# Gated delta rule and FP4 feed-forward layer: the triangular matrices of the chunk solve change layout by 32x32 block transposes on VectorE instead of over DRAM

## The chip, the cores and the metric

The kernel runs on one core of a Trainium2 chip. The metric is the time on the device in microseconds (us) of one execution; lower is better. A core has five engines with a queue of instructions each: TensorE (PE, matrix products; its weight loads are PEld), VectorE (DVE), ScalarE (ACT), GpSimd (POOL) and SyncE (SP, which here only issues DMAs). Each works through its queue in order; semaphores tie them together.

## What is computed

The reference takes x of shape (2, 4096, 512), normalizes each row, and adds to x the outputs of two branches. The first is an attention of 16 heads with a gated delta rule, a recurrence over 4096 steps; the second a feed-forward part with FP4 weights:

```python
def step(S, inp):
    q_t, k_t, v_t, g_t, b_t = inp
    S = S * jnp.exp(g_t)[..., None, None]
    mem = jnp.einsum('bhk,bhkv->bhv', k_t, S)
    delta = (v_t - mem) * b_t[..., None]
    S = S + jnp.einsum('bhk,bhv->bhkv', k_t, delta)
    o_t = jnp.einsum('bhk,bhkv->bhv', q_t, S)
    return (S, o_t)
...
h = jax.nn.silu(gate) * up
y = jnp.einsum('bsi,hi->bsh', h, w_down)
rms = jnp.sqrt(jnp.mean(y * y, axis=-1, keepdims=True) + EPS)
...
xn = _layernorm(x, axis=-1)
x = x + _L0_attn_ref(xn, ...) + _L0_ffn_ref(xn, ...)
```

Before the recurrence, q, k and v pass a causal convolution of 4 taps and a SiLU, q and k are scaled to unit length, and g and beta come from x by small projections. After it, o is normalized per head, gated, and multiplied by o_w.

## The kernel before

A **tile** is 128 positions of both batch entries (NB = 2), so there are 32 tiles. Within a tile the recurrence is done in 4 chunks of 32 positions (CH = 32, NC = 4). For each of the 2 x 4 x 16 = 128 combinations of batch entry, chunk and head there is a 32 x 32 unit triangular matrix, and its inverse T is needed. The inverses are computed on GpSimd with one of the 128 combinations on each partition.

The work is a software pipeline over tiles. One **step** of each engine does the front of a tile n (projections, convolution, keys, gram products, solve, the whole feed-forward part) and the rest of the recurrence for the tile t before it. `run` gives every engine the same steps: the first has no t, the last, the 33rd, has no n. Each engine's order within a step is written out by hand.

The path of the triangles, with the lines of the profile:

- TensorE forms the gram products `gram(0)` and `gram(1)` (L1354). VectorE's `gram_products(b)` multiplies them with the decays: L987 writes the matrix for the solve into `kbq` (signal a_done), L988 writes D. Here a partition holds one position j of a chunk, and along the row are the 16 heads and 32 positions i: the **row layout**.
- SyncE writes kbq to DRAM, `scr_a` (L393), and reads it back into `la` in pieces of 16 partitions (L399), 2 x (1 + 4) issues per tile. In `la` a partition is one combination of batch entry, chunk and head, and holds the whole 32 x 32 matrix: the **head layout**.
- GpSimd's `solve` (L494 to L515) clears `lt`, waits for la, and does 31 steps of a product (L511) and a subtraction (L515). Its last signals t_done. Behind it in GpSimd's queue is `feed_forward_scale` (L525, L527), which turns ScalarE's sums of squares (L813) into the scale yr.
- SyncE writes lt to `scr_t` (L411) and reads it into `tT`, back in row layout (L417), 1 + 8 issues per tile.
- TensorE's `t_times_r` (L1221) of the next step uses tT as weights. It waits for the reads (t_read) and for out_done.

`la`, `tT` and the half `knq[1]` share the first 1024 columns of the tile `arena`; `lt` and `qk_rows` share the next 1024.

In the feed-forward part TensorE computes units u = 0 to 21 (L1153, L1154) and then products `down(m)` (L1166). ScalarE takes a unit from PSUM (L613), VectorE adds three scaled parts to it (L893, three per unit), ScalarE applies SiLU (L624), VectorE multiplies (`hidden`, L905). TensorE's unit(u) waits with its first half until VectorE's second L893 of unit(u-2) is done, with its second half for the third. Units 0 to 4 are interleaved with the gram products. At the end of a step VectorE forms the result in `obuf` (L1071, once per batch entry, after yr), which signals out_done, and begins the next step with the copy of the halo (L995), for which ScalarE's L600 waits, and behind that L593, which empties the banks of TensorE's projections (L1122).

## Time and profile before

| | before |
|---|---|
| median of 3 runs | 3328.89 us |
| lowest and highest | 3327.97, 3332.89 us |
| span of the profiled execution | 3330.7 us |
| TensorE busy | 3142.1 us (94%) |
| VectorE busy | 2390.6 us (72%) |
| GpSimd busy | 1918.8 us (58%) |
| ScalarE busy | 1667.4 us (50%) |
| chain that ended last | TensorE 77%, VectorE 12%, issue 6%, GpSimd 2%, DMA 1% |

The span goes from the first to the last instruction of the profiled execution; its own time was not given apart from it. It lies 1.8 us above the median of the runs. "Busy" on TensorE is occupancy, not its peak rate. Idle time of an engine costs something only if another one that is late waits for it.

### The profile page before, as it was taken

To read this page: it belongs to the slowest core of one execution; us is meant where nothing else is said; L and a number is where in the kernel's file an instruction comes from. 1 tells how busy PE (TensorE), PEld (TensorE's weight loads), DVE (VectorE), ACT (ScalarE), POOL (GpSimd) and SP (SyncE) were. 2 spreads that over 40 slices of the span, in tenths; PEclk is the share of its full clock that TensorE was granted. 3 is DMA by queue.
4 is the path that set the end of the run, shared out by engine and by line. 5 is a ranking of instruction groups with operands and counts; after the bars stand their busy time and mean duration, and the time that the engine had idled before them with its cause. 6 is when DMAs were issued, how large, how long until landed. Compare 5 with 4: busy or idle time off the path is not lost.

```text
span 3330.7 us, 118645 instructions
## 1 busy us (share of the span) xinstructions
PE 3142.1 (94%) x45632; PEld 2252.9 (68%) x45632; DVE 2390.6 (72%) x5408; ACT 1667.4 (50%) x3306; POOL 1918.8 (58%) x2865
## 2 busy tenths in 40 slices
PE   5999999999999999999999999999999999999995
PEld 4666766766666766666767767667667666767663
DVE  7677776777776777777777767777767777767772
ACT  3544554544554545554445545445545455544452
POOL 4566555666555665556665556665556655556652
PEclk8999999999999999999999999999999999999996
DMA  3111111111111111111111111111111111111111
GB/s 112 39 46 27 37 43 33 46 45 28 34 43 36 46 37 27 43 37 42 46 27 37 43 33 46 46 27 37 43 33 46 40 28 39 42 37 46 34 25 30
DMA packets 318318, 132.08 MB, mean 40 GB/s; under 512 B 277089, under 2 KB 278881, under 8 KB 317793
## 3 DMA queue, kind: packets, MB, share of 16 engines
q1 hardware_dynamic: 313824, 119.26, 14.3%
q8 instruction: 383, 6.28, 0.8%
q10 hardware_dynamic: 4096, 6.42, 0.5%
q14 instruction: 15, 0.11, 0.0%
HBM read 75.30 MB, written 50.33 MB: 38 GB/s over the span
## 4 chain that ended last, share of the span: by engine, by line
PE 77%; DVE 12%; issue 6%; POOL 2%; ACT 1%; ACTq 1%; DMA 1%; DVEq 0%; SPq 0%; POOLq 0%
PE PS L1166 17%; PE PS L1122 13%; PE PS L1153 8%; PE PS L1235 7%; PE PS L1154 7%; PE PS L1376 6%; DVE arena L893 4%; PE PS L1221 3%; PE PS L1300 2%; PE PS L1253 2%; DVE arena L378 2%; PE PS L1271 2%; PE PS L1391 2%; DVE arena L988 1%; PE PS L1178 1%
## 5 line engine op out<-in xcount | busy, mean ns | idle before, releaser
L893 DVE SCALAR_TENSOR_TENSOR arena<-PS,sc,arena 128x256 f32<-128x256 f32 x2112 | 1001.0, 482 | 253.0 <-ACT arena L613 152.2
L1153 PE MATMUL PS<-xh,wgu 128*128 128x256 f32 x2816 | 871.6, 341 | 35.9 <-DVE arena L893 35.4
L613 ACT ACTIVATE arena<-PS,sc 128x256 f32<-128x256 f32 x704 | 330.0, 474 | 759.0 <-PE PS L1154 700.3
L1154 PE MATMUL PS<-xl,wgu 128*128 128x256 f32 x2816 | 698.8, 282 | 0.0
L1166 PE MATMUL PS<-wdn,inner 128*128 128x512 f32 x1408 | 650.7, 592 | 0.0
L1153 PEld LDWEIGHTS PS<-xh,wgu 128*128 128x128 f32 x2816 | 531.2, 189 | 155.8 <-issue 84.2
L511 POOL TENSOR_TENSOR work<-arena 128x31 f32<-128x31 f32 (+15 forms) x992 | 511.9, 516 | 137.5 <-DMA arena<-scr_a 62.3
L515 POOL TENSOR_TENSOR arena<-arena,work 128x31 f32<-128x31 f32 (+15 forms) x992 | 542.1, 546 | 77.7
L1154 PEld LDWEIGHTS PS<-xl,wgu 128*128 128x128 f32 x2816 | 530.4, 188 | 83.2 <-issue 83.2
L1122 PE MATMUL PS<-xnT,wqkv 128*128 128x256 f32 x2048 | 485.6, 388 | 25.2 <-ACT inner L593 15.4
L1122 PEld LDWEIGHTS PS<-xnT,wqkv 128*128 128x128 f32 x2048 | 383.6, 192 | 93.1 <-ACT inner L593 16.4
L877 DVE SCALAR_TENSOR_TENSOR qkv<-inner,cw,qkv 128x256 f32<-128x256 f32 x768 | 398.8, 557 | 55.9 <-ACT qkv L600 46.7
L1166 PEld LDWEIGHTS PS<-wdn,inner 128*128 128x128 f32 x1408 | 245.5, 189 | 199.8 <-issue 199.4
L1235 PE MATMUL PS<-wg,xnT 128*128 128x512 f32 x512 | 264.8, 621 | 0.0
L1376 PE MATMUL PS<-wo,arena 128*128 128x512 f32 x512 | 242.0, 596 | 0.0
L378 POOL TENSOR_TENSOR R<-arena,ckg 128x256 f32<-128x256 f32 x64 | 57.3, 913 | 314.1 <-DVE ckt L959 314.1
L632 ACT ACTIVATE ub<-PS 32x512 f32<-32x512 f32 x256 | 136.7, 580 | 202.2 <-PE PS L1253 197.6
L905 DVE TENSOR_TENSOR inner<-arena,sg 128x256 f32<-128x256 f32 x352 | 203.4, 585 | 30.5 <-DVE arena L893 0.5
L624 ACT ACTIVATE sg<-arena 128x256 f32<-128x256 f32 x352 | 145.2, 413 | 154.1 <-DVE arena L893 153.8
L915 DVE TENSOR_TENSOR tmp<-PS,bdmask 128x128 f32<-128x128 f32 x256 | 74.1, 289 | 206.2 <-PE PS L1271 201.8
L533 POOL TENSOR_TENSOR arena<-arena 128x512 f32<-128x512 f32 x64 | 80.4, 1278 | 226.3 <-ACT qkv L776 226.3
L1071 DVE SCALAR_TENSOR_TENSOR obuf<-PS,yr,obuf 128x512 f32<-128x512 f32 x64 | 45.1, 745 | 217.6 <-POOL yr L527 217.6
(147 smaller groups left out, 4619.2 us busy)
## 6 DMA issues: line engine op xcount, KB each, us to landing
xt<-in_x SPq DMA_DIRECT2D x64, 256.0 KB, 2.8
scr_a<-arena SPq DMA_DIRECT2D x64, 256.0 KB, 2.4
arena<-scr_a SPq DMA_DIRECT2D x256, 64.0 KB, 3.2
obuf<-in_x SPq DMA_DIRECT2D x64, 256.0 KB, 2.8
scr_t<-arena SPq DMA_DIRECT2D x32, 512.0 KB, 2.7
arena<-scr_t SPq DMA_DIRECT2D x256, 64.0 KB, 2.3
out<-obuf SPq DMA_DIRECT2D x64, 256.0 KB, 2.0
wqkv<-in_wqkv ACTq DMA_DIRECT2D x1, 2048.0 KB, 14.3
```

What stands on the lines that cost most here:

```text
L511: eng.tensor_tensor(pr, la[:, j, j + 1:].unsqueeze(1).broadcast_to([P, w, r]), bc(lt[:, 0:w, j], r), ALU.mult).then_inc(solve_part.sem, 1)
L515: eng.tensor_tensor(tail, tail, pr, ALU.subtract).then_inc((t_done if j == CH - 2 else solve_part).sem, 1)
L613: eng.activation(fa[:, u % 4, :], PS[:, bank(u, 0), 0:NB * P], ACT.Copy, scale=sc[:, u % 2, KB * m:KB * m + 1]).then_inc(fa_scaled.sem, 1)
L877: eng.scalar_tensor_tensor(out=acc, in0=cin[:, mm, :, k:k + P], scalar=cw[:, mm, k:k + 1], in1=acc, op0=ALU.mult, op1=ALU.add).then_inc((t ...
L893: eng.scalar_tensor_tensor(out=fa[:, u % 4, :], in0=PS[:, bank(u, k // 2), k % 2 * NB * P:][:, 0:NB * P], scalar=sc[:, u % 2, KB * m + k:K ...
L905: eng.tensor_tensor(inner[:, m, :], fa[:, (2 * m + 1) % 4, :], sg[:, m % 2, :], ALU.mult).then_inc(h_done.sem, 1)
L1122: ins = eng.matmul(PS[:, proj_bank(m), 0:NB * P], wqkv[:, kb, m * P:(m + 1) * P], xnT[:, kb, :], start=(kb == 0), stop=(kb == KB - 1))
L1153: eng.matmul(o, w, xh[:, k, :], start=True, stop=False)
L1154: ins = eng.matmul(o, w, xl[:, k, :], start=False, stop=True)
L1166: ins = eng.matmul(PS[:, b, :], inner[:, m, b * P:(b + 1) * P], wdn[:, m, :], start=(m == 0), stop=(m == FM - 1))
L1235: ins = eng.matmul(PS[:, 4 + b, :], xnT[:, kb, b * P:(b + 1) * P], wg[:, kb, :], start=(kb == 0), stop=(kb == KB - 1))
L1376: ins = eng.matmul(PS[:, 6 + b, :], oT[b][:, kb, :], wo[:, kb, :], start=(kb == 0), stop=(kb == KB - 1))
```

## The change

The two DRAM tensors and the 19 DMA issues per tile around them go. In their place VectorE gets two instructions per tile, each a transpose of all 32 x 32 blocks (32 partitions by 32 elements) of a tile of 128 x 1024 f32: `turn_a` from kbq to la, placed behind gram_products(1), and `turn_t` from lt to tT, placed behind the last hidden(m) and ahead of the result. In both, the element next to each on a partition lies 32 elements (128 bytes) on, in the source and in the destination. A partition of la then holds another combination of batch entry, chunk and head than before; the solve treats all alike, and turn_t turns it back.

```diff
-    scr_a = nc.dram_tensor("scr_a", (NB, NC, CH, H, CH), F32).ap()
-    scr_t = nc.dram_tensor("scr_t", (NB, NC, H, CH, CH), F32).ap()
...
-            if n:
-                for b in range(NB):
-                    hold(eng, *a_done.at(n, b + 1))
-                    eng.dma_start(scr_a[b].rearrange("c j h i -> (c j) (h i)"), kbq[:, b, :]).then_inc(a_written.sem, 16)
-                    hold(eng, *a_written.at(n, 16 * (b + 1)))
-                    if b == 0:
-                        hold(eng, *gram_out.at(n, NB))
-                    for c in range(NC):
-                        p0 = (b * NC + c) * H
-                        eng.dma_start(la[p0:p0 + H, :, :],
-                                      scr_a[b, c].rearrange("j h i -> h j i")).then_inc(a_read.sem, 16)
...
-            hold(eng, *t_done.at(n, 1))
-            eng.dma_start(scr_t[:, :, :, :, :].rearrange("b c h j i -> (b c h) (j i)"),
-                          arena[:, 1024:2048]).then_inc(t_written.sem, 16)
-            hold(eng, *t_written.at(n, 16))
-            for b in range(NB):
-                for c in range(NC):
-                    s = slice(c * CH, (c + 1) * CH)
-                    eng.dma_start(tT[s, b, :, :], scr_t[b, c].rearrange("h j i -> j h i")).then_inc(t_read.sem, 16)
...
             if not n.first:
-                hold(eng, *t_written.at(n.before(), 16))
+                hold(eng, *t_turned.at(n.before(), 1))
...
-            hold(eng, *a_read.at(n, 16 * NB * NC))
+            hold(eng, *a_turned.at(n, 1))
...
+            def turn_a():
+                if not n:
+                    return
+                eng.wait_ge(*a_done.at(n, NB))
+                eng.wait_ge(*gram_out.at(n, NB))
+                eng.transpose(la.rearrange("p j i -> p i j"),
+                              kbq[:, :, :].rearrange("p b (h i) -> p i (b h)", i=CH)).then_inc(a_turned.sem, 1)
+
+            def turn_t():
+                eng.wait_ge(*t_done.at(n, 1))
+                eng.transpose(tT.rearrange("p b h i -> p i (b h)"),
+                              lt.rearrange("p j i -> p i j")).then_inc(t_turned.sem, 1)
...
             gram_products(1)
+            turn_a()
             unit(3)
...
+            turn_t()
             eng.wait_ge(*res_loaded.at(n, 16 * NB))
...
-                    hold(eng, *t_read.at(t, 16 * NB * NC))
+                    hold(eng, *t_turned.at(t, 1))
```

On VectorE, behind the gram products, the queue of a middle step reads as follows before the change (L987 and L988 are gram_products(1), L893 is unit(3) and unit(4), L905 is hidden):

```order
L987 TENSOR_TENSOR arena<-PS,arena 128x4x2x64
L988 TENSOR_TENSOR arena<-PS,arena 128x4x2x64
L886 REGISTER_ALU
L893 SCALAR_TENSOR_TENSOR arena<-PS,sc,arena 128x256
L889 REGISTER_ALU
L893 SCALAR_TENSOR_TENSOR arena<-PS,sc,arena 128x256 x2
L901 ISA
L905 TENSOR_TENSOR inner<-arena,sg 128x256
L901 REGISTER_ALU
L905 TENSOR_TENSOR inner<-arena,sg 128x256
```

And with the change, where the same code has lower line numbers (L977 and L978 are gram_products(1), L957 is turn_a, L870 is a unit, L882 is hidden):

```order
L977 TENSOR_TENSOR arena<-PS,arena 128x4x2x64
L978 TENSOR_TENSOR arena<-PS,arena 128x4x2x64
L957 STREAM_TRANSPOSE arena<-arena 128x32x32
L863 REGISTER_ALU
L870 SCALAR_TENSOR_TENSOR arena<-PS,sc,arena 128x256
L866 REGISTER_ALU
L870 SCALAR_TENSOR_TENSOR arena<-PS,sc,arena 128x256 x2
L878 ISA
L882 TENSOR_TENSOR inner<-arena,sg 128x256
```

The transpose has come in between the gram products and unit(3); all that stood behind keeps its order.

At the end of the same step, before:

```order
L905 TENSOR_TENSOR inner<-arena,sg 128x256
L1067 REGISTER_ALU
L1071 SCALAR_TENSOR_TENSOR obuf<-PS,yr,obuf 128x512 x2
L372 REGISTER_ALU
L372 COMPARE_AND_BRANCH
L995 COPY inner<-halo 128x16x3
```

And with the change (L962 is turn_t, L1063 the result):

```order
L882 TENSOR_TENSOR inner<-arena,sg 128x256
L962 STREAM_TRANSPOSE arena<-arena 128x32x32
L1059 REGISTER_ALU
L1063 SCALAR_TENSOR_TENSOR obuf<-PS,yr,obuf 128x512 x2
L368 REGISTER_ALU
L368 COMPARE_AND_BRANCH
L985 COPY inner<-halo 128x16x3
```

The second transpose stands ahead of the two instructions of the result and the next step's copy of the halo, in a place where VectorE had no work of its own.

## Rows read from the trace of the kernel before

**Rows 1.** The page, part 4: the chain that ended last, shares by engine.

```profile
PE 77%; DVE 12%; issue 6%; POOL 2%; ACT 1%; ACTq 1%; DMA 1%; DVEq 0%; SPq 0%; POOLq 0%
```

**Rows 2.** Waits: waiter, what it waited for: us in total, times, longest.

```profile
POOL work L511 <- DMA arena<-scr_a: 62.3, 32, 20.3
...
PE PS L1153 <- DVE arena L893: 35.4, 97, 0.5
...
PE PS L1122 <- ACT inner L593: 15.4, 2, 10.9
...
PE PS L1221 <- DMA arena<-scr_t: 10.6, 1, 10.6
```

**Rows 3.** Timeline, VectorE, middle tile: start us, us, engine, line, operation, [idle before].

```profile
1699.61 0.68 DVE L988 TENSOR_TENSOR arena<-PS,arena 128x512 f32<-128x512 f32 x1
1700.21 1.58 DVE L893 SCALAR_TENSOR_TENSOR arena<-PS,sc,arena 128x256 f32<-128x256 f32 x3
...
1702.38 3.09 DVE L893 SCALAR_TENSOR_TENSOR arena<-PS,sc,arena 128x256 f32<-128x256 f32 x6
```

**Rows 4.** Timeline, TensorE, the two halves of unit(6) of that tile.

```profile
1702.91 0.38 PE L1153 MATMUL PS<-xh,wgu 128*128 128x256 f32 x1 [0.45 <-DVE arena L893]
...
1704.02 0.39 PE L1153 MATMUL PS<-xh,wgu 128*128 128x256 f32 x1 [0.37 <-DVE arena L893]
```

**Rows 5.** Timeline, GpSimd, the first multiplication of that tile's solve.

```profile
1710.15 0.24 POOL L511 TENSOR_TENSOR work<-arena 128x31 f32<-128x31 f32 x1 [1.64 <-DMA arena<-scr_a]
```

**Rows 6.** Timeline, all engines, end of that tile and start of the next.

```profile
1747.48 0.27 POOL L515 TENSOR_TENSOR arena<-arena,work 128x31 f32<-128x31 f32 x1
1747.98 0.19 POOL L525 TENSOR_SCALAR yr<-ys 128x2 f32<-128x2 f32 x1 [0.24 <-ACT arena L813]
...
1749.17 1.41 DVE L1071 SCALAR_TENSOR_TENSOR obuf<-PS,yr,obuf 128x512 f32<-128x512 f32 x2 [6.65 <-POOL yr L527]
...
1750.33 7.15 PE L1122 MATMUL PS<-xnT,wqkv 128*128 128x256 f32 x32
...
1757.41 0.88 PE L1221 MATMUL PS<-R,arena 32*32 32x48 f32 x64
```

**Rows 7.** Timeline, all engines, the first tile and the start of the second.

```profile
86.57 1.58 DVE L893 SCALAR_TENSOR_TENSOR arena<-PS,sc,arena 128x256 f32<-128x256 f32 x3
...
95.93 0.24 POOL L511 TENSOR_TENSOR work<-arena 128x31 f32<-128x31 f32 x1 [20.31 <-DMA arena<-scr_a]
...
126.37 0.19 ACT L813 ACTIVATION_READ_ACCUMULATOR arena<-PS 128x1 f32 x1
...
129.11 3.70 PE L1122 MATMUL PS<-xnT,wqkv 128*128 128x256 f32 x16
133.78 0.19 POOL L525 TENSOR_SCALAR yr<-ys 128x2 f32<-128x2 f32 x1
...
137.35 5.41 PE L1122 MATMUL PS<-xnT,wqkv 128*128 128x256 f32 x16 [4.54 <-ACT inner L593]
...
142.94 0.88 PE L1221 MATMUL PS<-R,arena 32*32 32x48 f32 x64 [0.18 <-issue]
```

**Rows 8.** Timeline, all engines, end of the last tile's front and last step.

```profile
3261.89 0.19 ACT L813 ACTIVATION_READ_ACCUMULATOR arena<-PS 128x1 f32 x1
...
3271.99 4.01 PE L1221 MATMUL PS<-R,arena 32*32 32x48 f32 x239 [10.63 <-DMA arena<-scr_t]
```

**Rows 9.** Groups by form: xcount | busy us, mean ns | idle before; L515 at two times.

```profile
L987 DVE TENSOR_TENSOR arena<-PS,arena 128x512 f32<-128x512 f32 x64 | 43.9, 686 | 3.0 <-PE PS L1354 1.2
L915 DVE TENSOR_TENSOR tmp<-PS,bdmask 128x128 f32<-128x128 f32 x256 | 74.1, 289 | 206.2 <-PE PS L1271 201.8
L1079 DVE MEMSET S<- 128x1024 f32 x1 | 0.9, 912 | 0.2 <-issue 0.2
...
L515 POOL TENSOR_TENSOR arena<-arena,work 128x31 f32<-128x31 f32 x1 | 0.3, 252 | 0.1
...
L515 POOL TENSOR_TENSOR arena<-arena,work 128x31 f32<-128x31 f32 x1 | 0.3, 268 | 0.1
```

More of the change, by code:

```diff
@@ L205, in build @@
         res_loaded = signal("res_loaded", 32)
-        a_written = signal("a_written", 32)
-        a_read = signal("a_read", 128)
-        t_written = signal("t_written", 16)
-        t_read = signal("t_read", 128)
+        a_turned = signal("a_turned", 1)
+        t_turned = signal("t_turned", 1)
         g_split = signal("g_split", 2)
@@ L937, in keep_rows @@
                 if t and b == 0:
-                    eng.wait_ge(*t_written.at(t, 16))
+                    eng.wait_ge(*t_turned.at(t, 1))
                 eng.tensor_copy(qk_rows[:, b, :], PS[:, 6 + b, :]).then_inc(qk_kept.sem, 1)
@@ L965, in products @@
                 if t and b == 0:
-                    eng.wait_ge(*a_written.at(t, 16 * NB))
+                    eng.wait_ge(*a_turned.at(t, 1))
                 if b == 0:
```

## The prediction

> **What bounds the kernel now.** I read the page first. The chain that ended last is 77% TensorE and 12% VectorE, with 1% for DMA [rows 1]. So a DMA round trip that goes is worth something only where TensorE waits for it. I looked for that in the waits [rows 2]. Over 32 tiles GpSimd waits 62.3 us for the reads from scr_a, once per tile, of which 20.3 us fall on one tile. TensorE waits for the reads from scr_t once in the whole run, for 10.6 us. And 97 times, three per tile, it waits for VectorE's line L893, 35.4 us in all, or 1.1 us per tile. One more wait stands out: TensorE for ScalarE's L593, 15.4 us in two waits only. Then I read one tile in the middle, in order of time [rows 3 to 6], the first tile [rows 7] and the last step [rows 8]. From the first L1221 of the second tile at 142.94 to that of the middle tile at 1757.41 there are 16 tiles, so one takes 100.9 us.
>
> The view of the middle tile decides the case. Behind its gram products VectorE starts one operation on another without idle time: L988, then the three L893 of unit(3) 0.60 us after it, later the six of unit(4) and unit(5) [rows 3]. TensorE stands behind them: at 1702.91 it had waited 0.45 us and at 1704.02 0.37 us, both for L893 [rows 4]. Its unit(u) asks for unit(u-2) of VectorE, and 1702.91 is 0.04 us after the end of the first L893 of unit(4) (1702.38 and 0.49 us). There VectorE sets the pace of the engine that is the bound.
>
> **The change, part by part.** (a) **turn_a**, one VectorE instruction of 128 x 1024 f32 per tile, goes exactly between L988 and unit(3). No row shows a transpose on VectorE, so I price it from neighbours [rows 9]. L915 with 128 elements takes 289 ns and L987 with 512 takes 686 ns, which is 1.03 ns per element. The start to start distance behind L988 is 0.60 us for 512 elements [rows 3]. So 1024 elements at one per cycle hold the next operation back by 0.60 + 512 x 1.03 ns = 1.13 us, and I add 0.04 us for 32 elements that a block must hold before it can be written: T = 1.17 us. The lower bound is 0.60 us, if it moves two elements at a time; the only row with 1024 elements on this engine, a memset without a source, takes 912 ns, which is less than 1024 x 1.03 ns, so more than one per cycle is seen. The upper bound is 2.24 us, if each element costs two cycles (another 1024 x 1.03 ns): both operands step by 32 elements, 128 bytes, from one element to the next, and no VectorE row here has such a step. GpSimd has one: the first L515 of a solve runs over 31 adjacent elements in 252 ns, the last over 31 elements 128 bytes apart in 268 ns [rows 9]. That is 0.52 ns per element; over 1024 elements it adds 0.53 us and makes T 1.70 us. I take 1.17 us, since the nearest rows by engine all run at one element per cycle, and keep 0.60 to 2.24 us.
>
> The Trainium skill (SBUF — State Buffer, section Specifications) says that SBUF has 16-byte lines, and that an access which goes to a new line each time pays a penalty. It speaks against this change: every element of both turns is on a new line. The GpSimd pair shows such a penalty, but a small one; no run here shows it for VectorE.
>
> Who pays T? Queued behind turn_a on VectorE are unit(3), hidden(0), hidden(1) and unit(4), with no idle time between them; TensorE already waits there, so its unit(6) starts T later, then unit(7) and all that is behind it. Nothing later in the tile gives it back: TensorE has no long wait in a middle tile, and ScalarE and VectorE are fed by it. So T counts in full in each of 32 tiles: 32 x 1.17 = **37.4 us lost**.
>
> (b) **The round trip over scr_a** goes. GpSimd's first L511 waited 1.64 us for it after its memset [rows 5]; it will find la ready and end its solve 1.64 us earlier, at about 1746.1. In a middle tile this buys nothing. The solve ended at 1747.75, and the next GpSimd instruction then waited another 0.24 us for ScalarE [rows 6]; so ScalarE, fed by the last down product of TensorE, is what comes last there.
>
> (c) **turn_t** waits on VectorE for the end of the solve. Queued behind it are the two L1071 of the result, which release out_done for TensorE, and then the copy of the halo. VectorE was idle for 6.65 us before L1071 [rows 6], so a turn of 1.2 us from 1746.1 is over by 1747.3, ahead of the 1749.17 + T at which L1071 can start. The cover is 4.2 us and costs nothing up to that length of a turn. Without the cover each further microsecond would push the next tile's halo copy, and then ScalarE.
>
> (d) **The round trip over scr_t** goes. In a middle tile TensorE starts L1221 at 1757.41, right where the 7.15 us of projections from 1750.33 end [rows 6]: the trip was hidden, the gain is nothing. In the last step nothing covers it: TensorE waited 10.63 us and started L1221 at 3271.99 [rows 8]. Now turn_t is over at about 3262.7. What is late next is out_done. ScalarE's last sum ended at 3262.08; with T added 3263.25; the square root on GpSimd and the start of L1071 follow as in a middle tile, 1.19 us after L525 (1747.98 to 1749.17), which itself comes some 0.2 us behind ScalarE. That is 3264.65, and 1.41 us later, at 3266.1, TensorE can start. It started at 3271.99 + T = 3273.16 if nothing else changed, so **7.1 us are gained**.
>
> (e) **The first tile.** There GpSimd had no older tile's work, so it waited 20.31 us for la and began the solve at 95.93; it ended just before L525 at 133.78, while ScalarE's last sum was there at 126.56 [rows 7]. The scale of the result came late from the solve, the halo copy behind it on VectorE too, and TensorE stood 4.54 us. From the start of the projections to L1221 it took 142.94 - 129.11 = 13.83 us, against 1757.41 - 1750.33 = 7.08 us in a middle tile. VectorE began unit(3) at 86.57; there turn_a now goes, so la is ready at 87.74 and the solve, 37.85 us long, ends at 125.6. ScalarE, T later, is there at 127.7 and comes last again, as in a middle tile, so **6.7 us are gained**.
>
> (f) SyncE loses 19 issues per tile, 10 around scr_a and 9 around scr_t. Its loads of x and stores of the result are no longer queued behind these, but none of them stands in [rows 2] or is waited for in [rows 3 to 6], so I cost this at nothing.
>
> The sum against the profiled execution is 37.4 - 7.1 - 6.7 = +23.6 us: its span of 3330.7 us becomes 3354.3. The median of the runs shown is 3328.89 us, 1.8 us below that span, so the time becomes 3352 us, 0.7% slower.
>
> **The rivals.** (1) **The 128-byte steps cost cycles.** For it: the GpSimd pair [rows 9]. Against it: that pair differs by 16 ns only, and GpSimd is another engine. With T = 1.70 us the sum is 54.4 - 13.8 = +40.6 and the time 3369 us; with T = 2.24 us it is 71.7 - 13.8 = +57.9 and 3387 us. The rule of the Trainium skill on lines of 16 bytes (SBUF — State Buffer, Specifications) would be this rival. (2) **The turn moves two elements per cycle.** This is the case on the other side. Its place is the gap between L988 and unit(3), its price is T = 0.60 us, and it decides as soon as T is under (13.8 + 6.7) / 32 = 0.64 us: the sum is 19.2 - 13.8 = +5.4, the time 3334 us, no change that can be measured. For it speaks the memset of 912 ns, against it that no reading instruction of VectorE here with more than 512 elements shows such a rate. (3) **TensorE does not pay T**, because its waits in [rows 4] really end with something else than VectorE, ScalarE's L613 for instance. Then only the gains are left: 3328.9 - 13.8 = 3315 us. Against it: the 0.04 us between VectorE's end and TensorE's start, and 97 such waits with none over 0.5 us. (4) **A turn of over 4 us**, as if the blocks were filled and emptied one after the other, each with a delay. Then turn_t sticks out as well and the time is over 3328.9 + 32 x 4.2 - 13.8 = 3449 us. Nothing speaks for it but the absence of a row.
>
> **How the numbers follow.** Chances: the forecast 0.54, with a range of its own from 3346 to 3360 us (T from 1.0 to 1.4 us); rival 1 0.27; rival 2 0.09; rival 3 0.05; rival 4 0.05. About 0.2%, 6.7 us, is what a measurement of this kernel can tell from no change. Faster is rival 3, 0.05. Same is rival 2 and a little of the forecast's low end, 0.10. The rest, 0.85, is slower. The range takes in the forecast and rival 1 to its far end, and leaves out most of rival 2, rival 3 and rival 4: 3340 to 3388 us.
>
> **What would show it.** In the profile of the changed kernel: the transposes as a group on VectorE of 64 with a mean near 1.2 us (2.2 us for rival 1, 0.6 us for rival 2); TensorE's waits for L893's successor up from 35.4 us to about 35.4 + 37.4 = 73 us over 97 times; a middle tile of 102.1 us instead of 101; VectorE's idle time before the result still 5 us or more; GpSimd's wait before its first multiplication gone; no wait of TensorE for L593's successor of some 5 us in the second tile; and TensorE's wait in the last step down from 10.6 to under 4 us. The prediction is wrong in its main step if the waits for L893's successor do not grow, and wrong in a size if they grow by another amount than the mean of turn_a times 32.

## The result and the profile after

The changed kernel takes 3396.59 us (median of 4 executions, 3395.27 to 3400.83) against 3328.43 us for the kernel before (4 executions, 3325.91 to 3332.89): 1.0207 times as long, 95% interval 1.0193 to 1.0222. That is slower, as forecast, but 45 us above the forecast of 3352 us and 9 us above the upper end of the range. The profiled execution took 3395.55 us with a span of 3393.7 us, 63.0 us more than the span before. The medians differ by 68.2 us: the profiled execution before is the slowest of its four (3332.89 us), the one after is close to the fastest of its own. The parts below are those of the two profiled spans.

Each tile has one instruction that starts by the same rule in both kernels, the first scaling of the result (line L525 before, L502 after), once ScalarE's last sum and the solve are done. I take it as the mark between tiles: it cuts the span into a head, 31 tiles and a tail. Its line in the view by source, before and then after (first and last start at the end):

```profile
L525 POOL TENSOR_SCALAR yr<-ys x32: 191/191/193, 133.8 to 3263.2; 128x2 f32<-128x2 f32 x32
```

```profile
L502 POOL TENSOR_SCALAR yr<-ys x32: 191/191/191, 126.9 to 3330.3; 128x2 f32<-128x2 f32 x32
```

So the 31 tiles took 3129.4 us before and 3203.4 us after, 100.95 and 103.34 us each: **74.0 us lost**. The head became 6.9 us shorter. The tail, from the last start to the end of the span, went from 67.5 to 63.4 us, 4.1 us shorter. Together 74.0 - 6.9 - 4.1 = 63.0 us.

The page after, part 1 and then the chain of part 4, beside [rows 1]. DMA is gone from the chain and VectorE has 15% of it instead of 12%:

```profile
PE 3166.6 (93%) x45632; PEld 2277.2 (67%) x45632; DVE 2497.1 (74%) x5472; ACT 1668.2 (49%) x3306; POOL 1925.6 (57%) x2865
...
PE 76%; DVE 15%; issue 7%; ACTq 1%; ACT 0%; DVEq 0%; POOL 0%; POOLq 0%
```

The two new groups on VectorE (count | busy us, mean ns | idle before them). L957 is turn_a, L962 is turn_t:

```profile
L957 DVE STREAM_TRANSPOSE arena<-arena 128x1024 f32<-128x1024 f32 x32 | 69.0, 2157 | 0.0
...
L962 DVE STREAM_TRANSPOSE arena<-arena 128x1024 f32<-128x1024 f32 x32 | 67.7, 2116 | 58.6 <-POOL arena L492 58.6
```

A turn takes 2.1 us, not 1.2. The waits that answer to [rows 2] (L1145 is the old L1153, L870 the old L893, L1063 the old L1071):

```profile
PE PS L1145 <- DVE arena L870: 90.8, 68, 2.6
...
POOL yr L502 <- ACT arena L790: 121.3, 32, 5.5
DVE obuf L1063 <- POOL yr L504: 90.8, 32, 4.5
...
POOL work L488 <- DVE arena L957: 11.6, 1, 11.6
```

TensorE's wait for the units' line went from 35.4 to 90.8 us, that is by 55.4 us, or 0.8 of the 69.0 us that the 32 turn_a take; the longest single one went from 0.5 to 2.6 us. GpSimd's last instruction now waits for ScalarE, 3.8 us per tile, so the solve has slack. GpSimd waits for turn_a once, in the first tile. The middle tile around turn_a, beside [rows 3], VectorE's timeline:

```profile
1727.06 0.68 DVE L978 TENSOR_TENSOR arena<-PS,arena 128x512 f32<-128x512 f32 x1
1727.66 2.14 DVE L957 STREAM_TRANSPOSE arena<-arena 128x1024 f32<-128x1024 f32 x1
1729.70 1.54 DVE L870 SCALAR_TENSOR_TENSOR arena<-PS,sc,arena 128x256 f32<-128x256 f32 x3
1731.16 0.75 DVE L882 TENSOR_TENSOR inner<-arena,sg 128x256 f32<-128x256 f32 x2
1731.82 1.58 DVE L870 SCALAR_TENSOR_TENSOR arena<-PS,sc,arena 128x256 f32<-128x256 f32 x3
```

From the start of turn_a to the next start are 2.04 us: this is T. TensorE in the same place, beside [rows 4]:

```profile
1729.52 0.28 PE L1145 MATMUL PS<-xh,wgu 128*128 128x256 f32 x1
...
1732.35 0.58 PE L1145 MATMUL PS<-xh,wgu 128*128 128x256 f32 x1 [2.44 <-DVE arena L870]
...
1732.95 0.41 PE L1145 MATMUL PS<-xh,wgu 128*128 128x256 f32 x1
```

It waits 2.44 us where it waited 0.45, and starts 0.04 us after the first L870 has ended (1731.82 and 0.49 us). And then something new: a product of the same line that took 0.28 us before the stall takes 0.41 us behind it. The view of stretches shows why (us, busy time and count of PE, PEld, DVE, ACT, POOL, then TensorE's granted clock as a share of full speed, and the DMA engines' share and GB/s):

```profile
1726.00:1729.00 3.00, 2.67 (x49) 2.30 (x35) 2.94 (x4) 1.52 (x3) 2.23 (x2) 1.00 0.03 5
1729.00:1732.00 3.00, 0.91 (x8) 0.71 (x6) 2.86 (x7) 0.34 (x1) 3.00 (x1) 0.99 0.00 0
1732.00:1735.00 3.00, 2.65 (x11) 2.47 (x12) 2.63 (x6) 2.64 (x6) 2.92 (x4) 0.50 0.00 0
1735.00:1738.00 3.00, 3.00 (x10) 1.97 (x10) 2.71 (x7) 1.08 (x3) 2.08 (x8) 0.50 0.00 0
1738.00:1741.00 3.00, 3.00 (x20) 2.25 (x18) 1.40 (x3) 0.47 (x1) 2.53 (x7) 0.88 0.00 0
```

TensorE was busy for 0.91 of 3 us, and then its granted clock is 0.50, the 1.2 GHz level, until some way into the last stretch shown. This happens behind the wait for the units in 19 of the 31 tiles. The tile shown is one of the four where it lasts longest; in all 19 it is 78.5 us at 0.50, or 4.1 us each. In the kernel before it happens behind the units in no tile, but once behind the stall of 4.54 us at the start of the second tile [rows 7]. The 19 tiles take 103.7 us on average, the others, the last of the 31 apart, 102.5 us. Another trace of it is PEld's busy time: 2277.2 us after, 24.3 us more than the 2252.9 us before, for the same 45632 weight loads.

So the 74.0 us are 31 x 1.6 us that every tile pays (50 us), 19 x 1.15 us behind the fall of the clock (22 us), and 2 to 3 us that the last of the 31 tiles is longer still (105.5 us). For 1.4 us of those TensorE pauses ahead of L1277, and the profile shows nothing that it waits for; why is open.

The end of a middle tile, beside [rows 6]:

```profile
1773.97 2.14 DVE L962 STREAM_TRANSPOSE arena<-arena 128x1024 f32<-128x1024 f32 x1 [0.16 <-POOL arena L492]
...
1779.39 0.19 POOL L502 TENSOR_SCALAR yr<-ys 128x2 f32<-128x2 f32 x1 [5.45 <-ACT arena L790]
1780.58 1.41 DVE L1063 SCALAR_TENSOR_TENSOR obuf<-PS,yr,obuf 128x512 f32<-128x512 f32 x2 [4.47 <-POOL yr L504]
...
1781.74 7.15 PE L1114 MATMUL PS<-xnT,wqkv 128*128 128x256 f32 x32
...
1788.82 0.88 PE L1213 MATMUL PS<-R,arena 32*32 32x48 f32 x64
```

turn_t starts at 1773.97 and the result at 1780.58, 6.61 us later, so turn_t stands in idle time with 4.47 us to spare, and TensorE's 7.08 us from L1114 to L1213 are what they were. The first tile beside [rows 7], and the last step beside [rows 8]:

```profile
126.94 0.19 POOL L502 TENSOR_SCALAR yr<-ys 128x2 f32<-128x2 f32 x1 [3.25 <-ACT arena L790]
...
129.28 7.15 PE L1114 MATMUL PS<-xnT,wqkv 128*128 128x256 f32 x32
...
136.36 0.88 PE L1213 MATMUL PS<-R,arena 32*32 32x48 f32 x64
```

```profile
3330.32 0.19 POOL L502 TENSOR_SCALAR yr<-ys 128x2 f32<-128x2 f32 x1 [2.94 <-ACT arena L790]
...
3333.07 4.19 PE L1213 MATMUL PS<-R,arena 32*32 32x48 f32 x240 [3.67 <-DVE obuf L1063]
```

The stall of 4.54 us in the second tile is gone: from the start of the projections to L1213 are 7.08 us instead of 13.83. In the last step TensorE waits 3.67 us, now for the result.

### The profile page after: what moved, and what is told of

Same layout as the page of the kernel before. It is cut to its first block, busy times and chain, and to the rows that moved or that the text cites. A ratio compares the mean times of both kernels' runs of the same rounds, so it can differ in the third digit from the quotient of the medians.

```text
span 3393.7 us, 117699 instructions
## 1 busy us (share of the span) xinstructions
PE 3166.6 (93%) x45632; PEld 2277.2 (67%) x45632; DVE 2497.1 (74%) x5472; ACT 1668.2 (49%) x3306; POOL 1925.6 (57%) x2865
## 4 chain that ended last, share of the span: by engine, by line
PE 76%; DVE 15%; issue 7%; ACTq 1%; ACT 0%; DVEq 0%; POOL 0%; POOLq 0%
PE PS L1158 18%; PE PS L1114 13%; PE PS L1145 8%; PE PS L1146 8%; PE PS L1368 7%; PE PS L1227 6%; DVE arena L870 4%; PE PS L1213 3%; DVE arena L957 2%; PE PS L1245 2%; DVE qkv L854 2%; DVE arena L374 2%; PE PS L1263 2%; PE PS L1383 2%; PE PS L1292 1%
## 5 line engine op out<-in xcount | busy, mean ns | idle before, releaser
L870 DVE SCALAR_TENSOR_TENSOR arena<-PS,sc,arena 128x256 f32<-128x256 f32 x2112 | 1001.7, 482 | 289.4 <-ACT arena L590 188.3
L1145 PE MATMUL PS<-xh,wgu 128*128 128x256 f32 x2816 | 892.8, 348 | 91.4 <-DVE arena L870 90.8
L1146 PE MATMUL PS<-xl,wgu 128*128 128x256 f32 x2816 | 718.9, 287 | 0.0
L1145 PEld LDWEIGHTS PS<-xh,wgu 128*128 128x128 f32 x2816 | 547.6, 194 | 210.3 <-DVE arena L870 110.0
L1158 PE MATMUL PS<-wdn,inner 128*128 128x512 f32 x1408 | 660.2, 599 | 0.0
L1146 PEld LDWEIGHTS PS<-xl,wgu 128*128 128x128 f32 x2816 | 547.8, 195 | 83.2 <-issue 83.2
L1114 PE MATMUL PS<-xnT,wqkv 128*128 128x256 f32 x2048 | 483.0, 387 | 19.2 <-ACT inner L570 10.5
L854 DVE SCALAR_TENSOR_TENSOR qkv<-inner,cw,qkv 128x256 f32<-128x256 f32 x768 | 398.8, 557 | 57.2 <-ACT qkv L577 48.1
L1114 PEld LDWEIGHTS PS<-xnT,wqkv 128*128 128x128 f32 x2048 | 382.3, 192 | 86.0 <-issue 15.4
L882 DVE TENSOR_TENSOR inner<-arena,sg 128x256 f32<-128x256 f32 x352 | 171.1, 493 | 30.5 <-DVE arena L870 0.5
L898 DVE SCALAR_TENSOR_TENSOR S<-S,exs,tmp 128x64 f32<-128x64 f32 x512 | 171.8, 377 | 9.0
```

Of the source, the lines that this page charges most:

```text
L854: eng.scalar_tensor_tensor(out=acc, in0=cin[:, mm, :, k:k + P], scalar=cw[:, mm, k:k + 1], in1=acc, op0=ALU.mult, op1=ALU.add).then_inc((t ...
L870: eng.scalar_tensor_tensor(out=fa[:, u % 4, :], in0=PS[:, bank(u, k // 2), k % 2 * NB * P:][:, 0:NB * P], scalar=sc[:, u % 2, KB * m + k:K ...
L898: eng.scalar_tensor_tensor(out=S[:, (c + 1) % NC, b, f, :], in0=S[:, c, b, f, :], scalar=exs[:, b, k:k + 1], in1=tmp[:, f, :], op0=ALU.mul ...
L1114: ins = eng.matmul(PS[:, proj_bank(m), 0:NB * P], wqkv[:, kb, m * P:(m + 1) * P], xnT[:, kb, :], start=(kb == 0), stop=(kb == KB - 1))
L1145: eng.matmul(o, w, xh[:, k, :], start=True, stop=False)
L1146: ins = eng.matmul(o, w, xl[:, k, :], start=False, stop=True)
```

## The experiments

The theory was that turn_a costs 2.04 us of VectorE's time where TensorE stands behind it, because its elements lie 128 bytes apart, and that the stall takes TensorE's clock with it. The rivals: turn_t has a share; what the change takes away matters too; a 4-byte transpose is slow in any layout. Twelve variants were run; this table holds what they showed. T is the distance from the start of the turn that was added among the units to the next start on VectorE. "Wait" is TensorE's for the units' line: us in all and the longest. "Half" is the number of the 31 tiles in which the clock falls to 0.50 behind the wait for the units; where another stall brings a fall, the text says so. PEld is its busy time. The mean tile is read from the scaling as above. The ratio is to executions of the kernel before on the same chip.

| kernel | T us | wait | half | PEld us | tile us | ratio (95%) |
|---|---|---|---|---|---|---|
| before | none | 35.4, 0.5 | 0 | 2252.9 | 100.95 | 1 |
| changed | 2.04 | 90.8, 2.6 | 19 | 2277.2 | 103.34 | 1.0207 (1.0193 to 1.0222) |
| e1 turn_t only | none | 35.6, 0.5 | 0 | 2252.7 | 101.14 | 0.9987 (0.9978 to 0.9996) |
| e2 before + full turn | 2.04 | 91.7, 2.5 | 22 | 2279.1 | 103.48 | 1.0233 (1.0218 to 1.0249) |
| e3 adjacent elements | 1.15 | 66.1, 1.7 | 20 | 2276.9 | 102.48 | 1.0111 (1.0095 to 1.0126) |
| e4 steps in the write | 1.85 | 89.2, 2.4 | 8 | 2263.2 | 102.73 | 1.014, one execution |
| e12 before + turn in pairs | 1.16 | 68.2, 1.6 | 14 | 2270.8 | 102.45 | 1.0131 (1.0114 to 1.0148) |
| p16 before + half turn | 1.03 | 63.6, 1.5 | 17 | 2275.7 | 102.48 | 1.0120 (1.0106 to 1.0135) |
| e5 behind hidden(2) | 1.99 | 73.5, 0.8 | 0 | 2250.2 | 102.57 | 1.0127 (1.0112 to 1.0143) |
| e8 in two halves | 1.02, 1.09 | 63.9, 1.5 | 13 | 2272.4 | 102.53 | 1.0135 (1.0118 to 1.0152) |
| e6 behind hidden(3) | 2.06 | 48.1, 0.5 | 0 | 2253.6 | 102.10 | 1.0103 (1.0087 to 1.0120) |
| e6 behind hidden(4) | 2.00 | 36.3, 0.5 | 29, elsewhere | 2293.2 | 106.61 | 1.0510 (1.0492 to 1.0527) |
| e9 turn_a in the first tile only | 2.03, once | 37.5, 2.6 | 0 | 2250.6 | 101.03 | 0.9958 (0.9945 to 0.9970) |
| e11 e9, turn_t behind the result | 2.06, once | 37.1, 2.6 | 1, elsewhere | 2254.2 | 102.33 | 1.0087 (1.0073 to 1.0101) |

### turn_t alone

```diff
-            hold(eng, *t_done.at(n, 1))
-            eng.dma_start(scr_t[...], arena[:, 1024:2048]).then_inc(t_written.sem, 16)
...
+            def turn_t():
+                eng.wait_ge(*t_done.at(n, 1))
+                eng.transpose(tT.rearrange("p b h i -> p i (b h)"),
+                              lt.rearrange("p j i -> p i j")).then_inc(t_turned.sem, 1)
```

> The kernel before with turn_t alone: scr_t goes, the trip over scr_a stays. Theory (the whole loss is turn_a: 2.04 us of the path in each tile, and the clock of TensorE that falls behind the longer stall): nothing is lost in a middle tile, since turn_t of 2.1 us lies in VectorE's idle time before the result; the last step gains about 4 us as the changed kernel did there; the first tile keeps its stall. Time 3324 us (3320 to 3327), ratio about 0.999. The groups: 32 transposes of 2.1 us; TensorE's waits for line L893's successor at 35 us as before; no middle tile with a granted clock of one half. Rival (turn_t has a share: it holds back the halo copy of the next tile and VectorE's bank accesses): over 3332 us, up to 3328 + 32 x 2.1 - 4 = 3391 us.

Measured: 3327.66 us against 3330.79 us, a ratio of 0.9987. The theory's 0.999 holds: turn_t has no share in the loss, and the small gain is the last step's. Its mean tile is 0.19 us longer, 5.9 us over the 31. Of these, 2.8 us are in the last tile (104.5 us against 101.7) and 0.9 us in the first, and the 29 tiles between take 0.07 us more each. The waits may explain these: GpSimd waits longer for scr_a here (97.6 us instead of 62.3), so that the solve ends last and turn_t of 2.09 us really stands between it and the result.

### The turn without the rest of the change

```diff
+            def spare_turn():
+                if not n:
+                    return
+                eng.wait_ge(*a_done.at(n, NB))
+                eng.wait_ge(*gram_out.at(n, NB))
+                eng.transpose(spare.rearrange("p j i -> p i j")[:, 0:32, :],
+                              kbq[:, :, :].rearrange("p b (h i) -> p i (b h)", i=CH)[:, 0:32, :]).then_inc(spare_done.sem, 1)
...
             gram_products(1)
+            spare_turn()
             unit(3)
```

> The kernel before with one more VectorE instruction: the same 128 x 1024 transpose as turn_a, at the same place, into a free part of the arena that nobody reads. Both round trips over DRAM stay, so it has turn_a's length and none of the change's gains. Theory (the length of the instruction and the clock that follows it are the whole loss): the middle tiles as in the changed kernel, +74 us, and nothing back in the first tile and the last step: 3328 + 74 = 3402 us, within 3395 to 3410. Rival (part of the loss comes from what the change takes away or moves: the solve that begins earlier and shares SBUF with VectorE, the DMAs that go): clearly under 3396 us, about 3328 + 32 x 2.04 = 3393 us or less, with few or no stretches of half clock.

Measured: 3406.17 us, ratio 1.0233; the theory had 3402. The waits of TensorE, the tiles with the fallen clock and the tile time are close to those of the changed kernel. One instruction, added to the kernel before, whose result nobody reads, brings the whole loss. It also shows what the gains are worth: 1.0233 - 1.0207 = 0.0026, or 9 us, where the spans gave 6.9 + 4.1 us; each of the two ratios has an interval of some 5 us to either side.

### Where the elements lie

```diff
-                eng.transpose(la.rearrange("p j i -> p i j"),
-                              kbq[:, :, :].rearrange("p b (h i) -> p i (b h)", i=CH)).then_inc(a_turned.sem, 1)
+                eng.transpose(la[:, :, :],
+                              kbq[:, :, :].rearrange("p b (h i) -> p (b h) i", i=CH)).then_inc(a_turned.sem, 1)
```

> The changed kernel with the same 32 x 32 blocks, but the elements of a block stand side by side: turn_a steps by one element in both operands, turn_t reads at steps of 128 bytes and writes side by side. The order in the triangles is thereby another, so what is computed from them is not the reference's. Theory (the 128-byte steps cost the second cycle per element, the term that the prediction had as its upper bound): turn_a takes 1.1 to 1.2 us, the path loses 32 x 1.1 instead of 32 x 2.04, the stall of TensorE is about 1.5 us, and the time is near the forecast made for T = 1.17 us, 3352 to 3358 us. turn_t tells whether a step on the reading side alone costs: 1.1 us if not, 2.1 us if so. Rival (a 4-byte transpose takes two cycles per element wherever its elements stand): turn_a stays at 2.16 us and the time at 3396 us.

> The changed kernel with 128-byte steps on one side only: turn_a reads the elements of a block side by side and writes them at steps of 128 bytes, turn_t has them side by side in both operands. The order in the triangles is another, so what is computed from them is not the reference's. Theory (it is the reading side that costs the second cycle, since turn_t with stepped reads and adjacent writes still took 1974 ns against 2093 with both stepped): turn_a near 1.2 us, turn_t near 1.1 to 1.2 us, time as with adjacent steps in both, 3364 to 3368 us. Rival (either side alone costs it): turn_a near 2.0 us and the time near 3393 us.

The groups of both turns, first with adjacent elements in turn_a and a stepped read in turn_t, then with a stepped write in turn_a and adjacent elements in turn_t:

```profile
L962 DVE STREAM_TRANSPOSE arena<-arena 128x1024 f32<-128x1024 f32 x32 | 63.2, 1974 | 103.2 <-POOL arena L492 103.2
...
L957 DVE STREAM_TRANSPOSE arena<-arena 128x1024 f32<-128x1024 f32 x32 | 39.5, 1234 | 0.0
```

```profile
L957 DVE STREAM_TRANSPOSE arena<-arena 128x1024 f32<-128x1024 f32 x32 | 64.1, 2003 | 0.0
...
L962 DVE STREAM_TRANSPOSE arena<-arena 128x1024 f32<-128x1024 f32 x32 | 39.9, 1246 | 86.6 <-POOL arena L492 86.6
```

Adjacent on both sides: 1234 and 1246 ns. Steps in the read alone: 1974 ns. Steps in the write alone: 2003 ns. Steps in both: 2116 and 2157 ns. The layout is the cause; my guess that only the read costs was wrong, since either side alone costs nearly all of it. The one execution of e4 took 3377.13 us and not the rival's 3393, with 8 tiles of fallen clock instead of 19. From start to start the adjacent turn takes 1.15 us, close to the prediction's T of 1.17. The time for it is 3365.93 us, though, and not 3352: the clock falls in 20 tiles here too, behind waits of 1.6 us, and those tiles take 102.7 us where the others, the last apart, take 101.9 us.

> The kernel before with the added transpose of 128 x 1024 at turn_a's place, into a part of the arena that nobody reads, but on both sides the elements of a block now come in adjacent pairs (8 bytes), with a hop of 256 bytes behind each pair. Theory (a step of 128 bytes costs because every element is a single hop; two neighbours at a time restore the rate): from start to start about 1.15 us as with fully adjacent elements, TensorE's waits for the units at 64 to 68 us, and the time like the added half turn's of 1.03 us, 3372 to 3382 us. Rival (any hop costs, whatever the length of the run): 2.0 us, 3406 us as with the full added turn; between the two if the price is per hop, half as many hops: 1.6 us and about 3390 us. Said apart from this: the Trainium skill (Vector Engine (DVE) Microarchitecture Reference, section Measured stream behaviour on trn2) has pairs of adjacent words at 1.065 ns per column where all three ports hop behind each pair, and 1.98 ns where all hop at every element.

```diff
+                eng.transpose(arena[:, 2048:3072].rearrange("p (c i e) -> p i c e", i=CH, e=2),
+                              arena[:, 3072:4096].rearrange("p (c i e) -> p i c e", i=CH, e=2)).then_inc(spare_done.sem, 1)
```

```profile
L982 DVE STREAM_TRANSPOSE arena<-arena 128x1024 f32<-128x1024 f32 x32 | 39.5, 1235 | 0.0
```

With pairs of neighbours and a hop of 256 bytes behind each pair the turn is as fast as with adjacent elements, 1235 ns, and the time is 3375.71 us, within the theory's 3372 to 3382. So a hop at every second element costs nothing, and what costs is an element that stands alone. The Trainium skill (Vector Engine (DVE) Microarchitecture Reference, section Measured stream behaviour on trn2) states this for another operation and hops of 4 KiB: 1.71 to 1.76 ns per column with single hops on the sources or the destination, 1.98 ns with hops everywhere, 1.065 ns with pairs. Here, from start to start over 1024 columns, it is 1.81 ns (write), 1.99 ns (both) and 1.13 ns (pairs). A lone element with a hop of 256 bytes was not run. That a longer hop does not by itself restore the rate rests on those rows of 4 KiB, and on no run here.

### A shorter turn at the same place

```diff
+                eng.transpose(spare.rearrange("p j i -> p i j")[:, 0:16, :],
+                              kbq[:, :, :].rearrange("p b (h i) -> p i (b h)", i=CH)[:, 0:16, :]).then_inc(spare_done.sem, 1)
```

> The kernel before with an added transpose of 16 of the 32 blocks, 128 x 512, at turn_a's place, into a part of the arena that nobody reads; both trips stay. About 1.1 us long, 1.0 us from start to start. Theory (the loss is the length of the instruction, once per tile, and on top the half clock in some tiles): 3331 + 32 x 1.0 = 3363 us without a stretch of half clock, up to 3376 us with 19 of them as in the run with adjacent elements (turn_a 1.23 us long). TensorE's waits for the units' line at about 65 us. Rival (under some length the delay is absorbed, as rival 2 of the prediction had it for 0.60 us): 3335 to 3350 us.

Measured: 3375.34 us against 3335.38 us, ratio 1.0120, at the upper end of what the theory had. Nothing is absorbed: with half the length the added waiting is half (28.2 us instead of 55.4 to 56.3), while the clock still falls in 17 tiles. The rival by which a short delay is absorbed is out, at least down to 1.03 us.

### The turn at other places

```diff
             gram_products(1)
-            turn_a()
             unit(3)
...
                 hidden(m)
+                if m == 2:
+                    turn_a()
```

> The changed kernel with turn_a not before unit(3) but behind hidden(2), that is, after the four hidden and two units that TensorE waits for most closely; the solve has slack for it, since the square root after it waited for ScalarE. Theory (what is paid is TensorE's wait, and it is paid where VectorE is behind): VectorE has made up its backlog a little by then, so TensorE's waits for the line of the units grow by less than 55 us, the stretches of half clock become fewer, and the time lies between 3330 and 3385 us. If VectorE is behind just as much there, the path loses 2.04 us in each tile again: 3396 us. If the solve becomes late instead, GpSimd's last instruction and the result's scale move and the tile grows by that: also 3390 us or more, with TensorE's wait for ScalarE's sums' successor and VectorE's L1063 for GpSimd grown.

> The changed kernel with turn_a behind hidden(3), two more units later than behind hidden(2). Theory: VectorE's backlog ends in the kernel before with the sixth group of units behind the gram products (first wait for ScalarE at 1716), so turn_a stands at its end and part of its 2.04 us falls into slack; no stretch of half clock; the solve ends 0.7 us later than ScalarE's sums, which the 7.15 us of projections cover. Time 3345 to 3368 us. Rival (the solve is what comes last from here on, and its delay counts in each tile): 3373 us or more, with the wait of VectorE's L1063 for GpSimd and of TensorE before L1213's successor grown.

> The changed kernel with turn_a behind hidden(4), where VectorE in the kernel before already waited 1.0 us of every 2.6 us for ScalarE. Theory: TensorE's waits for the line of the units fall back to about 35 us; but the solve starts about 9 us later than behind hidden(2), where it had 2.8 us left before ScalarE's sums, so the scale of the result comes about 6 us late; the projections of the next tile cover most of that. Time 3320 to 3350 us. Rival (the late solve costs in full): 3328 + 31 x 6 = 3500 us at the worst, 3373 us or more in any case.

> The changed kernel with turn_a as two instructions of 16 blocks each, 1.03 us long, one behind hidden(1) and one behind hidden(3). Theory (a delay is paid at its length where VectorE is behind, and the clock falls only behind a stall of TensorE of more than about 1.5 us at one place): no stretch of half clock; the first half is paid in full, 32 x 1.0 us, the second in part; 3345 to 3365 us. Rival (the pieces add up to the same delay wherever they stand): 3373 us as with the whole behind hidden(2).

Behind hidden(2) the time is 3373.20 us, 23 us less than the change, and the clock falls in none of the 31 tiles: the longest wait is 0.8 us. But the mean tile of 102.57 us is that of the changed kernel's tiles with an unfallen clock, 102.5 us. So the length is still paid where it stands; what this place saves is the clock. This separates the two terms: 50 us of the 74 for the length, 24 us (31 x 0.77) for the clock, beside the 22 us that the changed kernel's own tiles gave.

Behind hidden(3) it is 3366.67 us. That lies in the theory's range of 3345 to 3368 us, but by luck, since the theory had the projections cover the late solve. TensorE's waits for the units grow by only 12.7 us, yet a tile is 1.15 us longer. The waits tell where the rest went:

```profile
DVE arena L962 <- POOL arena L492: 212.0, 32, 11.2
POOL work L488 <- DVE arena L957: 135.4, 32, 22.2
```

Besides 22.2 us in the first tile, GpSimd waits 3.7 us per tile for turn_a. VectorE then waits 6.6 us per tile for the solve, turns, and only behind that scales the result, with no idle time left in front of it (L1064 has none). Behind hidden(4) this decides everything (L1115 is the projection, L570 ScalarE's copy behind the halo; below it the chain that ended last, now 31% GpSimd):

```profile
PE PS L1115 <- ACT inner L570: 121.6, 33, 8.8
...
PE 34%; POOL 31%; DVE 19%; issue 12%; POOLq 2%; ACT 1%; DVEq 1%; ACTq 1%
```

The time is 3502.01 us: TensorE loses 3.8 us per tile at the start of the next one, and its clock falls there, in 29 tiles. I had expected 3320 to 3350 us, on the ground that the projections cover a late solve. They do not: they are themselves behind the halo copy, which is behind the result on VectorE. My rival for that run had it right.

The two halves behind hidden(1) and hidden(3) gave 3377.08 us: the first half stands where the waits are long (1.5 us) and the clock falls in 13 tiles. The expectation of no fallen clock was wrong; I had set the point from which it falls too high. No price of the fall shows here, though: these 13 tiles take 102.0 us and the others, the first and the last apart, 102.7 us. What slows this variant is, as behind hidden(3), in part a late solve. GpSimd waits 142.0 us for the second half, 20.8 of them in the first tile, and VectorE 197.2 us for the solve. The rival's 3373 us is near, but its reason, that the pieces add up to the same delay, isn't shown by this.

### What can be kept of the change

```diff
-                        eng.dma_start(la[p0:p0 + H, :, :],
+                        eng.dma_start((scr_b if n.first else la)[p0:p0 + H, :, :],
...
+                if not n or not n.first:
+                    return
+                eng.transpose(la.rearrange("p j i -> p i j"), ...).then_inc(a_turned.sem, 1)
```

> turn_t in every tile as in the run with turn_t alone, and turn_a in the first tile only; every other tile keeps its trip over scr_a. (In the first tile the reads of that trip go into a spare DRAM tensor that nobody reads.) Theory (the gains of the change are its first tile and its last step, the loss is turn_a in the middle tiles): against the kernel before the first tile gives back about 6 us, the last step 4 to 7 us, one T of 2 us is paid: 3331 - 4 - 6 = 3321 us, ratio 0.997 (0.995 to 0.9985), a version that beats both. In the profile: the first scale of the result at about 127 us instead of 134, no wait of TensorE of several us for ScalarE's L570's counterpart in the second tile. Rival (the second tile's start or something behind it gives the first tile's gain back): 3328 us, as with turn_t alone.

3322.06 us against 3335.38 us, 0.9958 (0.9945 to 0.9970): faster than both kernels, by 0.4% against the one before, a little more than the theory's 0.9970. Its scaling runs from 129.6 us on, 4.2 us earlier than before:

```profile
L520 POOL TENSOR_SCALAR yr<-ys x32: 191/192/193, 129.6 to 3261.5; 128x2 f32<-128x2 f32 x32
```

> The version with turn_a in the first tile only, and turn_t now behind the two instructions of the result instead of ahead of them. It tests what turn_t costs where the solve ends last: in that version VectorE waits for the solve, turns (2.1 us) and only then multiplies the result, which in the kernel before began 1.2 us after the solve. Theory (that delay is covered by the 7.15 us of projections, and moving the turn only shifts it in front of the next tile's halo copy): no difference that can be measured, ratio to the kernel before 0.9958 again (0.994 to 0.9975), and in the last step the result starts 2.1 us earlier but the transposed triangle ends as late. Rival (the result's release or the store behind it counts in each tile): up to 1 us per tile, ratio 0.987. Rival (the halo copy behind the turn counts, since ScalarE's convolution inputs wait for it): 32 x 1 to 2 us lost, ratio 1.005 to 1.015.

```diff
-            turn_t()
             eng.wait_ge(*res_loaded.at(n, 16 * NB))
...
                 eng.scalar_tensor_tensor(out=obuf[:, b, :], ...).then_inc(out_done.sem, 1)
+            turn_t()
```

The time is 3361.25 us, ratio 1.0087: 1.3 us more per tile, for moving one instruction behind the two of the result. Of its three forecasts the last holds, 1.005 to 1.015: the halo copy is late. Here are TensorE's row for it, 59 waits here and 5 in the version above (12.1 us), and the chain that ended last, where GpSimd has 31% instead of the 5% of the version above:

```profile
PE PS L1133 <- ACT inner L588: 28.9, 59, 6.5
...
PE 34%; POOL 31%; DVE 9%; issue 9%; DMA 9%; ACT 3%; SPq 3%; POOLq 2%; ACTq 1%; DVEq 0%
```

The row accounts for 16.8 of the 40 us. By the chain the round from the solve over the result, the turn, the halo copy and the next tile's front back to the solve now sets the pace; how the other 23 us divide over it is not shown.

## Why the prediction was right and wrong

- **Who pays for turn_a: right.** The place was read from [rows 3] and [rows 4]. TensorE's waits grew by 55.4 us to 90.8 us, where 73 us were forecast, and for T from 1.03 to 2.04 us the waits follow the length. By the prediction's own sign, growth by the mean of turn_a times 32, it should have been 69 us; it is 0.8 of that.
- **The price of turn_a: wrong, the main step.** It was T = 1.17 us from "the nearest rows by engine all run at one element per cycle"; it is 2.04 us. The rate was right for what those rows are, instructions with adjacent elements: e3 gives 1.15 us. The 128-byte steps cost the other 0.9 us. I had this as rival 1 with 0.27 and gave too much weight to the GpSimd pair of [rows 9], 16 ns apart, which is another engine. Between the changed kernel and e3 lie 3396.6 - 3365.9 = 31 us, two thirds of the miss.
- **The fall of the clock: missed.** No term stood for it. It is 22 us in the changed kernel, and it is why even e3, with the T that I forecast, is 14 us over 3352. Rows of the kernel before could have warned. In the second tile [rows 7] sixteen projections take 3.70 us ahead of the stall of 4.54 us and 5.41 us behind it, and in the last step TensorE stands still for 10.63 us [rows 8]. I had looked at the length of these stalls, and not at the granted clock (third figure from the end) behind them, the first line below for the second tile and the others for the last step:

```profile
138.00:141.00 3.00, 3.00 (x9) 2.37 (x8) 2.75 (x10) 2.62 (x5) 0.00 (x0) 0.50 0.75 117
...
3262.00:3265.00 3.00, 0.00 (x0) 0.00 (x0) 0.63 (x1) 2.97 (x4) 1.77 (x6) 0.91 0.35 141
...
3271.00:3274.00 3.00, 2.01 (x101) 2.04 (x105) 0.00 (x0) 0.00 (x0) 0.00 (x0) 0.50 0.04 6
```

Since rival 1 lacked this term too, the range ended at 3388 us. Such stalls are longer than those of turn_a, so even these rows did not show that 2.4 us would be enough.
- **T counts in full: nearly.** Where both trips stay, a tile whose clock stays up grew by 1.8 us for a T of 2.04 (e2), 1.1 us for 1.16 (e12) and 1.2 us for 1.03 (p16). Without the trips it grew by 1.6 us for 2.04 (changed kernel) and 1.0 us for 1.15 (e3). So some 0.2 us per tile comes back through what the change takes away, and up to 0.2 us more is not paid at all. Which part of it does so is not settled.
- **turn_t hidden: right** (e1). In the tile shown there are 6.61 us from its start to the result, where the forecast had 4.2 us of cover, and 4.47 us of them are left behind the turn. What I had not priced is its order with the result: e11 shows 1.3 us per tile for the other order.
- **The first tile: right.** 6.7 us were forecast from the stall of the projections, and it went from 13.83 to 7.08 us, 6.75 us less. T was to be paid in the first tile too and did not show: the projections begin at 129.28 instead of 129.11 us. Why is open.
- **The last step: right in its place, too large in the span.** L1213 starts 2.75 us behind the last scaling instead of 8.8 us, 6 us earlier; the tail is only 4.1 us shorter. The runs with the trip still in have tails of 64.0 to 64.4 us (e2, p16, e12), so some 3 us of the 67.5 us were this one execution's; e1, with turn_t alone, has 60.5 us. So 7.1 us was too much, and 1 to 4 us is what the runs bear out.
- **SyncE's issues at nothing: right to 0.2 us per tile.** e2 keeps them all, and its tiles with an unfallen clock take 102.8 us against 102.5 us.

The terms can be put together with what was measured; since they come from the same trace as the total, this is bookkeeping and no test. With T at 2.04 us the prediction's own sum is 65.3 - 13.8 = +51.5 us of span. Add 22 us for the clock, 2 us for the last of the 31 tiles and 3 us that the last step gave less; take off 13 us for 0.4 us per tile not paid and 2 us for the first tile, where T did not show: +63.5 us, against 63.0 us measured.

## What to carry over

Before an instruction is put on an engine for its count of elements, look at the steps of its operands: lone 4-byte elements on either side of this transpose cost nearly as much as on both, and pairs restored the rate. Where the bounding engine follows another closely, a delay of 1 to 2 us was paid nearly in full, and TensorE's clock could fall behind it, so the price of a stall is its length plus what the engine runs like afterwards. A change that is bad on average can have places where it is good: the first tile and the last step, where nothing covers the trip, were worth keeping.

## What the runs showed of the hardware

- A 128 x 1024 f32 block transpose on VectorE takes 1234 ns with adjacent elements, 1235 ns with pairs, 1974 to 2003 ns with a 128-byte step on one side, 2054 to 2157 ns with steps on both (means of a group).
- TensorE's clock fell to the 1.2 GHz level behind waits for the units of 1.4 to 2.5 us, in 8 to 22 of 31 tiles. Where these waits were 0.8 us at most, it fell behind them in none. Other stalls brought it down too: 4.54 us at the start of the second tile (kernel before), 3.4 to 3.6 us at the start of 29 tiles (hidden(4)), and a pause of 1.7 us in the last tile (e4, e11). Each tile with a fall behind the units has some 1.3 us more of weight loading (24.3 us for 19 tiles) and was 1.0 to 1.15 us longer with the full turn (changed kernel, e2) and 0.5 to 0.8 us longer with the short ones (p16, e12, e3). Which tiles it hits isn't told by the length of the wait: e4 waits 2.2 us in a middle tile and has 8 of them, e3 waits 1.6 us and has 20. That stays open.
- PEld's busy time marks this better than PE's, which rose by 18.6 us in e5 with no fallen clock at all, since the ends of matmuls are modelled.
